# Output stage of a Mamba/attention hybrid: three loads of the next batch moved in among the loads of z

## The reference, cut to what matters

```python
y = local_reverse(ys[0], row windows) + local_reverse(ys[1], column windows) \
  + local_reverse(ys[2] backwards) + local_reverse(ys[3] backwards)
y = layer_norm(y) * silu(z)
x = shortcut * skip_scale + y @ out_proj.T
h = conv3x3(gelu(conv3x3(layer_norm(x))))
x = x * skip_scale2 + h * sigmoid(relu(mean(h) @ ca1.T) @ ca2.T)
t = tokens(x)
t = t + linear_attention(layer_norm(t))
t = t + quantised_ffn(layer_norm(t))
```

## Time and profile before

| | us |
|---|---|
| median of three runs | 12572.94 |
| lowest, highest run | 12563.75, 12574.37 |
| profiled execution, its own time | 12557.75 |
| its span | 12555.9 |
| VectorE busy in the span | 11159.5 (89%) |
| POOL busy | 9784.8 (78%) |
| PE busy | 8741.3 (70%) |
| ScalarE busy | 7090.2 (56%) |
| L1427, 56 instructions: busy, idle before them | 135.4, 1145.3 |
| y loads (L912) in the phase of outputs, median to landing | 15.9 |

### The profile page before, as it was taken

One profiled execution on the slowest core, in us unless ns is written; L12 is line 12 of the kernel. 1 busy time (PEld: TensorE's weight loads), 2 busy tenths in 40 slices (PEclk: granted clock), 3 DMA queues, 4 the chain that ended last, 5 costly groups with the idle time before them and its releaser, 6 DMA issues. The chain is left out here.

```text
span 12555.9 us, 114737 instructions
## 1 busy us (share of the span) xinstructions
PE 8741.3 (70%) x25368; PEld 2451.3 (20%) x25368; DVE 11159.5 (89%) x7214; ACT 7090.2 (56%) x9476; POOL 9784.8 (78%) x4212
## 2 busy tenths in 40 slices
PE   8866666666666666666666666666666666588887
PEld 2321111111111111111111111111111111122223
DVE  7769999999999999999999999999999999554544
ACT  6755555555555555555555555555555555355555
POOL 0039999999999999999999999999999999212120
PEclk9977777777777777777777777777777777788888
DMA  3368877887777888887887788777788887433341
GB/s 105 110 161 181 180 180 177 180 181 178 177 179 178 179 178 180 181 180 179 180 181 180 179 180 181 177 177 179 179 179 179 183 181 169 101 90 91 78 98 30
DMA packets 569217, 2013.47 MB, mean 160 GB/s; under 512 B 82134, under 2 KB 87030, under 8 KB 553974
## 3 DMA queue, kind: packets, MB, share of 16 engines
q1 hardware_dynamic: 568566, 2006.60, 70.2%
HBM read 1599.46 MB, written 406.85 MB: 160 GB/s over the span
## 5 line engine op out<-in xcount | busy, mean ns | idle before, releaser
L823 POOL TENSOR_TENSOR dBu<-rep,BC 128x1024 f32<-128x1024 f32 x3072 | 7160.1, 2358 | 843.8 <-DMA rep<-dd_dram 831.7
L620 PE MATMUL py<-hC,fold 128*32 128x512 f32 x12288 | 2950.0, 859 | 2597.2 <-POOL hC L830 2454.5
L668 ACT ACTIVATE pd<-rep,a_now 128x1024 f32<-128x1024 f32 x3072 | 3420.9, 1114 | 1230.3 <-DVE hC L791 999.3
L783 DVE TENSOR_TENSOR_SCAN pd<-pd,carry,dBu 128x1024 f32<-128x1024 f32 x1536 | 3596.1, 2341 | 0.0
L830 POOL TENSOR_TENSOR hC<-h,BC 128x1024 f32<-128x1024 f32 x1024 | 2404.3, 2348 | 353.3 <-DVE h L783 314.5
L791 DVE TENSOR_TENSOR hC<-pd,BC 128x1024 f32<-128x1024 f32 x2048 | 2508.1, 1225 | 159.9 <-DVE pd L783 26.2
L783 DVE TENSOR_TENSOR_SCAN h<-pd,carry,dBu 128x1024 f32<-128x1024 f32 x768 | 1798.0, 2341 | 0.0
L680 ACT ACTIVATE carry<-pd 128x1 f32<-128x1 f32 x1536 | 262.5, 171 | 2702.5 <-DVE hC L791 2683.5
L620 PEld LDWEIGHTS py<-hC,fold 128*32 128x32 f32 x12288 | 519.5, 137 | 4796.9 <-POOL hC L830 2929.0
L783 DVE TENSOR_TENSOR_SCAN pd<-pd,dBu 128x1024 f32<-128x1024 f32 x512 | 1167.8, 2281 | 17.1 <-issue 7.6
L1427 POOL TENSOR_TENSOR p_y<-p_y 96x1024 f32<-96x1024 f32 x56 | 135.4, 2447 | 1145.3 <-DMA p_y<-y_dram 1145.3
(11 more groups left out here) (152 smaller groups left out, 8762.2 us busy)
## 6 DMA issues: line engine op xcount, KB each, us to landing
rep<-dd_dram SPq DMA_DIRECT2D x1024, 768.0 KB, 12.2
BC<-bc_dram SPq DMA_DIRECT2D x2048, 256.0 KB, 9.2
u<-u_dram SPq DMA_DIRECT2D x128, 768.0 KB, 5.4
dd_dram<-LG SPq DMA_DIRECT2D x256, 384.0 KB, 4.4
dd_dram<-RL SPq DMA_DIRECT2D x256, 384.0 KB, 3.0
y_dram<-y SPq DMA_DIRECT2D x256, 384.0 KB, 11.7
p_y<-y_dram SPq DMA_DIRECT2D x61, 1536.0 KB, 15.9
u_dram<-p_u SPq DMA_DIRECT2D x32, 1536.0 KB, 7.6
```

The source lines that it names most:

```text
L620: last = mm(py[32 * g:32 * g + 32, t2(t)], fold[:, :], hC[:, j % 2 * 3 + g, t2(t)], start=(j % 4 == 0), stop=(j % 4 == 3), skip_group_chec ...
L668: go(pd[:, i % 2, :], rep[:, half, 0, g, :], ACT.Exp, scale=a_now[:, i:i + 1]).then_inc(S.exped, 1)
L783: v.tensor_tensor_scan(turned(dst, k), turned(pd[:, i % 2, :], k), turned(dBu[:, i % 4, :], k), carry[:, i:i + 1] if c else 0.0, ALU.mult, ...
L823: nc.gpsimd.tensor_tensor(dBu[:, i % 4, :], rep[:, half, 1, g, :], BC[:, s, 0, r, :], ALU.mult).then_inc(S.dbu, 1)
```

## The change

`load_y_first` keeps the loads of directions 0 and 2 and their wait on `acc_made`. The load of direction 1 becomes a function of its own, `load_y_second`. For the first half of the next batch the former is called in the z loop behind the issue of z3, and the latter behind the issue of z5; before, all three followed z7. The order for the second half is as before. The number and size of the transfers, and every other engine's stream, are the same. The loads in front of the batch loop, for batch 0, are not touched.

```diff
             def load_y_first(b, h):
-                n = b * 2 + h
-                sp.wait_ge(S.acc_made, done(n * NT))
+                sp.wait_ge(S.acc_made, done((b * 2 + h) * NT))
                 load_y(b, h, 0, Y[:, 0, :], S.y_loaded0)
                 load_y(b, h, 2, Y[:, 2, :], S.y_loaded2)
+
+            def load_y_second(b, h):
                 load_y(b, h, 1, Y[:, 1, :], S.y_loaded1)
...
                 for t in range(NT):
                     sp.wait_ge(S.gated, done(b * NT + t - 1))
                     sp.dma_start(Z[:, t % 2, :, :], a.zs[b, :, :, tile(t)]).then_inc(z_loaded[t % 2], 16)
+                    if more and t == 3:
+                        load_y_first(b + 1, 0)
+                    if more and t == 5:
+                        load_y_second(b + 1, 0)
                 if more:
-                    load_y_first(b + 1, 0)
                     load_y_last(b + 1, 0)
                     load_y_first(b + 1, 1)
+                    load_y_second(b + 1, 1)
                     load_y_last(b + 1, 1)
```

## The result

| | before | changed |
|---|---|---|
| median, us | 12571.96 (12563.75 to 12574.37) | 12648.58 (12645.66 to 12659.07) |
| span of the profiled execution, us | 12555.9 | 12643.8 |

The changed kernel takes 1.0064 times as long (95% interval 1.0046 to 1.0081), 77 us more: slower, as forecast, and 3.6 us beyond the upper end of the range. From L912 on its lines stand later; on VectorE and POOL by 5: the gate is L1360 now (was L1355), x1 is L1338 (L1333), the sums are L1432 and L1438 (L1427 and L1433), the turns L1305 (L1300), x2 is L1375 (L1370). On PE the centring of x is L1011 (L1006).

What follows compares the result with a forecast made beforehand. The prediction took PE, in sequence through the output stage's y/z/x part, as the bound. Stall 3.8, tile 7's gate 1.4 and clock 0.8 made 6.0 us per batch, times 7 = 42, added to 12572.94: 12615 us, range 12575 to 12645.

Steps and rivals of the forecast that it cites:

- No gain from an earlier y: Output stage: y's lateness is covered by VectorE's 20.7 us wait for att, so loading it earlier gains 0.
- Part 1: SP's load queue: z4 queues behind y0 and y2 and lands 2.6 us late for tile 4's gate.
- Part 2: Tile 4's gate on VectorE: POOL's addition holds its pair, 5.5 us late, so PE stalls 3.8 us per batch.
- the first link: Tile 4's gate: z4 late in the queue, without POOL's hold; PE stalls 1.0 us per batch.
- Part 3: Tile 7's gate: POOL's second addition catches the second instruction of its pair, 1.4 us per batch, ends 0 and 3.5.
- the end of 3.5: Tile 7's gate: upper end, both halves of the pair caught by POOL's second addition, 3.5 us.
- Part 4: PE's clock behind the 3.8 us stall: may fall to half speed, costing 2.3 us; a third taken, 0.8 per batch.
- Part 5: y's second half: POOL's L1433 starts 1.7 us before the first x2 and covers it; no term in the sum.
- The small gain that I had left out: First x2 beside POOL's second-half sum: between 0.1 and 1.0 us a batch gained, left out of the sum.
- (b): Rival, y/z/x part: everything collides, clock falls each batch, tile 7's gate fully caught; 9.6 per batch, 12640 us; chance 0.25.
- (a): Rival, tile 4's gate: not held by POOL, only z4 late; 1.0 per batch, 7 us, 12580 us; chance 0.17.
- The batch period: Output stage, x2 to x2 (L1370 to L1370) over two periods: from 218.4 us to about 224.4.

Runs made afterwards that it cites:

- e3: Kernel before with only y's direction 1 load early, behind z5, directions 0 and 2 behind z7 as before: 12569.52 us, 1.0002 times before.
- e6: Changed kernel with z4 in its own place, issued ahead of y, and POOL's next-batch sums waiting for all eight gates: 12569.56 us, 1.0001 times before.
- e5: Changed kernel with z4 given its own place in hc_image and issued right behind z3, ahead of y: 12613.88 us, 1.0045 times before.
- e9: Kernel before, loads unmoved, plus four extra POOL sums per batch from tile 3's gate on, each reading two different tensors: 12599.38 us, 1.0024 times before.
- e1: Changed kernel, but POOL starts the next batch's sums only after all eight tiles are gated, loads still early: 12589.25 us, 1.0019 times before.
- e4: Changed kernel plus matmuls nobody reads on PE ahead of the centring of x of tiles 3 and 6, where it stalls: 12626.10 us, 1.0051 times before.
- e2: Changed kernel with y's direction 1 load put back behind z7, directions 0 and 2 still early: 12618.86 us, 1.0045 times before.
- e8: Kernel before plus five matmuls nobody reads in PE's gap ahead of the second convolution's third tile: 12553.00 us, 0.9988 times before.
- e7: Kernel before, loads unmoved, plus four extra POOL sums per batch from tile 3's gate on, reading one tensor twice: 12573.65 us, 1.0008 times before.

## Why the prediction was right in direction and too small

- **No gain from an earlier y: right.** L1305's wait is gone and reappears in full as L1375's wait for att (37.15 us). e3 and e6 move loads and gain nothing.
- **Part 1, z4 behind y: right.** POOL started 18.57 us behind z3's issue (forecast 18.7), and tile 4's gate waited to 11308.70, where the forecast, moved by 30.45, says 11308.85.
- **Part 2, POOL holds the gate: right, a little small.** The pair took 4.20 us, as worked out, and e5 and e9 show the hold without the late z. The stall was put at 3.8; PE's gap was 4.2 in the mean and the delay of x1 4.4. I let L1006 wait for L1333 alone; it also waits for the scaling of x that stands right behind it in VectorE's order (L1343 now), 0.6 us more. The same omission goes with the first link, 1.6 instead of 1.0 in e1. That L1355 would behave as L1370 was an inference between two instructions of one form; it held to a hundredth of a microsecond (a held second half takes 2.82 us). L1338 with one operand in PSUM stayed at 0.73 us in the middle of L1432. The Trainium skill (SBUF — State Buffer, SBUF: two separate sides) has the shared port pair as an exclusive lock between GpSimd and a VectorE instruction with two SBUF inputs. By that rule, too, the gate is held and L1338 isn't; the trace agrees.
- **Part 3, tile 7's gate: a failed size.** 1.4 forecast, 2.7 measured. I had the gate at 11299.4 and the second sum at 11299.8. In before's time L1438 started at 11299.14 and the gate, 6.05 us late, at 11301.79, so that both halves were held. This is the end of 3.5 that I had named and not taken. The order hung on 0.4 us, and both sides erred: the sum alone, 0.7 us sooner, would have stood ahead of the gate as forecast. The fall of the clock, which moved the gate further, wasn't needed: in the five batches of e4 where it held, the stall was as large (2.8 to 3.0). e2 shows it from the other side, since a later sum misses the gate altogether.
- **Part 4, the clock: the step that failed.** I gave it 0.8 us once. It was 2.2 behind the first stall and came a second time behind the second stall, 2.3 by the table, some 1.8 of that above what e2 and e4 have at that place (0.6 and 0.5). I took a third of the cost because the gap was shorter than the one in rows 10; the clock fell in all seven batches. And I priced a clock for one stall only, where part 3 makes another and brings the fall that every batch has near tile 7 forward by some microseconds. 0.8 against 4.5 (4.0 with what e2 and e4 have taken off) is most of the missing 5.6 us per batch (11.6 - 6.0); part 3 gives 1.3 and part 2 0.6. That the two clock terms are the clock, and not something else behind a stall, is what e4 shows.
- **Part 5: right in place.** The second half's L1438 started 1.2 us before the first x2 (forecast 1.7). The small gain that I had left out didn't come: the pair took 4.42 us in batch 2, where it took 4.12, and 5.0 in the mean of seven batches, where it took 4.3.
- **Rivals.** (b), everything collides, at 9.6 per batch, was the likelier case, and its own sum lacked the second fall of the clock. (a) is what e1 shows once POOL's part is taken out, at 1.6 and not 1.0 per batch.
- **The batch period**, L1370 to L1370, was to go from 218.4 us to about 224.4. From L1375 at 10942.05 to 11402.87 are two periods of 230.4: 12.0 more instead of 6.0.

## What to carry to other kernels

A load that comes early also brings its consumer forward: before moving it, ask which instructions will then run beside that consumer, here POOL's sums beside VectorE instructions with both tensors in SBUF. Delays in a full pipeline are chained: each moves the next meeting and may bring down PE's clock. Where the forecast hangs on an order that is decided by less than a microsecond, take the bad end of that term. If nobody waits for the data (here 20 us of cover), leave the load where it is.

## What the runs showed of the hardware that I had not expected

How long PE stood still didn't by itself decide whether the granted clock fell from 1.00 to 0.50. Behind the first gaps of the changed kernel, 3.8 to 5.0 us, it fell in seven of seven batches; behind those of e5, 1.8 to 2.9 us and with another of 0.7 us just after, also in seven of seven; behind those of e9, 2.2 us, in one of seven; behind those of e1, 0.8 to 2.1 us, in none. What else decides is not shown. Matmuls whose result is not read, put into such a gap, paid: 17 to 22 us in e4, 13 in e8. And a POOL sum of 96x1024 that reads one tensor twice is shorter than one that reads two: 1.89 us in e7 against 2.35 in e9, with VectorE out of the way; beside a held VectorE instruction one of e9 takes 2.79.
